# Expert stage of a graph layer with routed experts: the products of a tile with w1 set ahead of the turn of the next tile

## What is computed

```python
def _L0_ffn_ref(x, enc_w, enc_b, sw_w, sw_b, w1, b1, w2, b2):
    xt = x.reshape(-1, d)                       # 16384 tokens, d = 384
    route_prob = softmax((xt @ enc_w + enc_b) @ sw_w + sw_b)
    route_prob_max = max(route_prob)
    onehot = one_hot(argmax(route_prob), 8)
    h = einsum('td,edr->ter', xt, w1) + b1      # 64 hidden units for each expert
    h = gelu(h) * onehot[..., None]
    out = (einsum('ter,erd->td', h, w2) + onehot @ b2) * route_prob_max[:, None]
    return out
x = x + _L0_ffn_ref(_layernorm(x), ...)
```

## Time and profile before

| what | value |
|---|---|
| median of 3 runs | 2161.38 us (2161.37 to 2163.28) |
| the profiled run | 2160.51 us |
| its span, first to last instruction | 2158.7 us |
| mean granted clock of TensorE | 0.987 |
| busy: PE, DVE, ACT, POOL | 97%, 77%, 69%, 65% |

### The profile page before, as it was taken

One profiled execution on the slowest core, in us unless ns is written; L12 is line 12 of the kernel. 1 busy time (PEld: TensorE's weight loads), 2 busy tenths in 40 slices (PEclk: granted clock), 3 DMA queues, 4 the chain that ended last, 5 costly groups with the idle time before them and its releaser, 6 DMA issues. The chain is left out here.

```text
span 2158.7 us, 56998 instructions
## 1 busy us (share of the span) xinstructions
PE 2091.0 (97%) x13580; PEld 2038.0 (94%) x13581; DVE 1656.5 (77%) x5452; ACT 1491.7 (69%) x3901; POOL 1413.0 (65%) x3348
## 2 busy tenths in 40 slices
PE   6999999999999999999999999999999999968997
PEld 5999999999999999999999999999999999957996
DVE  5777777777777777677777777777777777758997
ACT  4777767667776776676776776677776767637775
POOL 2556666666666666666666666666666666655887
PEclk9999999999999999999999999999999999978999
DMA  7101111211111111111111111111111111117995
GB/s 194 32 27 50 38 49 48 104 50 47 43 49 50 51 42 50 43 47 47 43 46 50 47 42 50 44 50 50 50 39 50 47 39 49 34 56 234 279 294 192
DMA packets 94261, 153.77 MB, mean 71 GB/s; under 512 B 17621, under 2 KB 70619, under 8 KB 93954
## 3 DMA queue, kind: packets, MB, share of 16 engines
q1 hardware_dynamic: 75844, 99.61, 16.0%
q0 software_dynamic: 17408, 50.62, 6.1%
q10 hardware_dynamic: 704, 0.10, 0.0%
HBM read 96.11 MB, written 57.32 MB: 71 GB/s over the span
## 5 line engine op out<-in xcount | busy, mean ns | idle before, releaser
L422 PE MATMUL bank<-wT_hi,hT_hi 128*128 128x384 f32 x2304 | 798.8, 347 | 11.3 <-issue 4.8
L424 PE MATMUL bank<-wT_hi,hT_lo 128*128 128x384 f32 x2304 | 774.2, 336 | 0.0
L423 PE MATMUL bank<-wT_lo,hT_hi 128*128 128x384 f32 x2304 | 773.1, 336 | 0.0
L422 PEld LDWEIGHTS bank<-wT_hi,hT_hi 128*128 128x128 f32 x2304 | 434.9, 189 | 20.5 <-ACT bank L622 12.4
L423 PEld LDWEIGHTS bank<-wT_lo,hT_hi 128*128 128x128 f32 x2304 | 435.2, 189 | 0.0
L424 PEld LDWEIGHTS bank<-wT_hi,hT_lo 128*128 128x128 f32 x2304 | 434.0, 188 | 0.0
L1173 POOL TENSOR_TENSOR hT_lo<-hT,hT_hi 128x384 fp32r<-128x384 f32 x256 | 261.5, 1022 | 22.9 <-ACT hT_hi L687 21.3
L682 ACT ACTIVATE hT<-bank 128x384 f32<-128x384 f32 x256 | 125.9, 492 | 203.0 <-PE bank L414 183.5
L658 ACT CAST right_hi<-bank 128x384 fp32r<-128x384 f32 x256 | 122.6, 479 | 173.9 <-PE bank L424 173.2
L1228 POOL TENSOR_SCALAR_AFFINE_SELECT deltaT_hi<-turned_hi 128x128 fp32r<-128x128 f32 x256 | 85.3, 333 | 211.8 <-ACT turned_hi L664 209.2
L414 PE MATMUL bank<-hT 128*128 128x128 f32 x1536 | 213.3, 275 | 0.0
(11 more groups left out here) (201 smaller groups left out, 5145.2 us busy)
## 6 DMA issues: line engine op xcount, KB each, us to landing
tok<-buckets SPq DMA_DIRECT2D x72, 388.0 KB, 4.5
x_in<-in_x_dram SPq DMA_DIRECT2D x128, 192.0 KB, 2.5
x_res<-in_x_dram SPq DMA_DIRECT2D x128, 192.0 KB, 2.4
adj_in<-in_adj_dram SPq DMA_DIRECT2D x128, 64.0 KB, 2.4
buckets<-pads SPq DMA_DIRECT2D x9, 388.0 KB, 4.9
out_dram<-out_rows,row_ids POOLq DMA_INDIRECT x144
buckets<-rows,dest_words POOLq DMA_INDIRECT x128, 2.7
w_top<-in_L_ffn_w_dram SPq DMA_DIRECT2D x2, 768.0 KB
```

What stands on the lines that cost most here:

```text
L422: pe.matmul(o, hi, w_hi, start=False, stop=False, skip_group_check=True)
L423: pe.matmul(o, hi, w_lo, start=False, stop=False, skip_group_check=True)
L424: last = pe.matmul(o, lo, w_hi, start=False, stop=(c == C - 1), skip_group_check=True)
```

## The change

In TensorE's step, the products of tile i-2 with w1 are issued ahead of the transposes of tile i-1. Nothing else differs.

```diff
                     def step(i, k):
+                        if there(i - 2):
+                            hidden(i - 2, k - 2)
                         if there(i - 1):
                             turn(i - 1, k - 1)
-                        if there(i - 2):
-                            hidden(i - 2, k - 2)
                         if there(i - OUTPUT):
                             output(i - OUTPUT, (k - OUTPUT) % RING)
```

## The result

The changed kernel takes **2191.2 us** (median of 4 runs, 2190.67 to 2192.34), the kernel before beside it 2161.44: a ratio of 1.0136, interval 1.0124 to 1.0148. So it is 29.8 us slower, where 20.8 had been worked out. The profiled run took 2191.17, 1.8 above its span.

What follows compares the result with a forecast made beforehand. TensorE ran its steps without a gap, and GpSimd's store queue set the end. Steps of 2.965 against 2.678 over 68, with filling +3.5, gave +23.0; less 2.18 for stores, +20.8 us, so 2182, range 2174 to 2195.

Steps and rivals of the forecast that it cites:

- What would show it: Signs expected in the profile after: TensorE gaps 0.2 to 0.3 us, turns 2.9 to 3.0 apart, GpSimd lag near 0.9.
- The first chain: Expert-stage loop: turn's end, ScalarE's copy, w1 load, six products, next turn, closed in itself; 2.91 us a step.
- the second chain: VectorE's order over two steps, from ScalarE's copy and gelu through cast, combine, normalise, last-third copy: 5.845, 2.92 a step.
- The release of the products: Latency from a copy's end to TensorE's load of w1: 0.07 us taken, bounds 0.00 and 0.25.
- My upper bound of 0.25: Rival: every release costs 0.25, not 0.07; step 3.134 us, time 2193.5; past 2194 without a falling clock, chance 0.06.
- The turn of the loop: VectorE's loss to issue once in eight tiles: 0.35 us per eight, 0.044 a step, hidden before, exposed after.
- The filling: Pipeline start of the expert stage: first combine at 1963.2 instead of 1959.70, +3.5 us, bounds +2.2 and +4.1.
- The store queue: GpSimd's scattered stores, 2.71 us a tile, had fallen back by 2.18 us, which a slower TensorE gets back.
- The third rival: Span's end doesn't move or comes earlier; stores alone would set it if steps stayed at 2.65; chance 0.04.
- The falling clock: Rival: TensorE's clock drops to its lower level in the loop; half the steps slow gives +66, near 2248; chance 0.03.

Runs made afterwards that it cites:

- the cast's other form: Changed kernel on chip 7 with VectorE's cast of the gelu's upper part written as a two-input maximum of the gelu with itself: 2194.37 us, ratio 1.0150.
- the kernel with two products: Kernel before, on chip 14, with the third of the three products with w1 (channels 256 to 383) left out: 2221.92 us, ratio 1.0026.

## Why the prediction was right, and where its sizes were off

**The mechanism was right.** Turn, copy and products of one tile became a closed path. The gaps, the gelu straight behind the copy, the cast waiting for the gelu and the clock at 1.00 are all in the rows after, as listed under "What would show it". The first chain of 2.91 is there to the hundredth: of the 64 distances between the turns of tiles 5 to 69, 8 are within 0.01 of 2.91 in the changed kernel on chip 7, and 21 in the one without writes. Three signs of that list came otherwise. The copies didn't end TensorE's gaps in equal numbers but 48 to 16, VectorE's the more, so the second chain was the longer by more than 0.01. The turns were not 2.9 to 3.0 apart but 3.08 in the median, from 2.91 to 3.50. And GpSimd waited for the combine in 16 places, not at all tiles; its lag was 0.83 at tile 68, as expected.

**The range held by some luck.** The time is 9 us above the sum and 3.8 below the upper end. That end was worked out for a release of 0.25 us on both chains. What came was 0.22 on one of them, and a stretched cast and a later filling, for which the range had only its 2 us.

**A step: 3.080, not 2.965.** The first two of these terms of the second chain were too small.
*The release of the products.* I took 0.07 for either copy, from a row with ScalarE's. Behind ScalarE's copy it is that, mostly 0.06 to 0.07. Behind VectorE's it is mostly 0.21 to 0.23, as in the rows above: 2041.05 to 2041.28 and 2044.00 to 2044.22. The chain passes it once in two steps, so with 0.22 it is +0.075 a step: 5.845 becomes 5.995, or 3.00 a step. My upper bound of 0.25, for which I gave 0.06, was nearer the mark for that engine, but I had charged it to both chains. The cause isn't shown. In the kernel's text the wait for ScalarE's copy stands ahead of this one, and the wait for the gelu of two tiles back behind it.
*The cast.* 0.296 before, 0.360 after: +0.032 a step by the halving that the cast's other form showed. Before, 40 of the 60 casts of tiles 5 to 64 started with no store under way and none was held by one to its end; now the cast starts right behind the gelu, 58 of 60 start inside a store, and 32 end just behind it, by up to 0.29 later than alone. In the rows above the store ends at 2044.86 and the cast, 0.45 long, at 2044.98. That a moved instruction may take longer was in no term of my sum.
*The turn of the loop.* I had 0.35 per eight tiles. What is left of the step is 3.080 - 3.00 - 0.032 = 0.048, or 0.38 per eight, which is near the 2.4 us in 7 places of the waits. This term is a remainder, so it takes up what is off in the other two as well.
Together 3.080 - 2.965 = 0.115 a step, 7.8 us over 68.

**The filling: 5.3 us, not 3.5.** The turn of tile 1 took 1.46 at the lower clock where I took 0.97; I had this 0.66 as the upper bound and 0.49 of it came. The rest, 1.2, is that the products of tile 0 started at 1952.80 instead of 1951.59. ScalarE's copy of tile 0 stands behind its normalise of tile 1, and that waited for its rows until 1950.73. Nothing that the change moves comes ahead of this load, so I put it down to the run; that is argued, not shown. The changed kernel without its writes speaks for it: there the products of tile 0 start at 1951.57, and the first combine comes at 1963.80, 0.6 behind my 1963.2, of which the slow turn is 0.5. On chip 7 the first combine comes at 1963.80 to 1966.29 in the three changed kernels and at 1962.28 in the kernel before without its writes, so from one profile to another this term varies by 2.5 us in either order.

**The store queue: 2.18 predicted, 2.23 given back.** This term held, and the kernel before without its writes, with the same lag, shows that it is the time in which GpSimd issues, not that of the writes. The end of the span says the same: it comes 16.9 us behind the combine of tile 68 before and 14.9 after. The third rival fell with its condition: steps didn't stay at 2.65.

**The falling clock** is refuted for this loop: steps of 2.91 to 3.50 us with 2.65 us of work in each left it at 1.00. The Trainium skill (TensorE: Matmul & The Clock Gate, A second HAM failure mode) tells of a kernel with short idle gaps and cycled banks in which it goes back and forth; here it doesn't.

**On chip 11** the same change costs 1.0024; on chip 14 the changed kernel itself wasn't run. Nothing in the prediction covered that: it took one chip's profile for the kernel's. The median distance of turns of the changed kernel is 3.20 us on chip 11 and 3.06 on chip 7, so its path is no shorter there. The kernel before loses 54 us on that chip and the changed one 30, so the order adds little there; how the held-up tiles share this out stays open with their cause.

## What to carry to other kernels

When two engines hand a tile back and forth, put a whole other piece of work between the hand-over and its use; to move the use up to the hand-over turns cover into a closed path, and the step is then the sum of that path, whatever each engine's share of busy time was. Follow the path over two steps as well as one: here the longer chain went through VectorE's queue and was found only by walking its order. And size each term for the place to which the change moves it, since a release by another engine and a cast beside a store each cost more there than in the rows of before.

## What the runs showed of the hardware

- **TensorE's load of w1 came later behind VectorE's copy than behind ScalarE's**: mostly 0.21 to 0.23 us after the end of the one (in 37 of 48 tiles of the result's profile) and 0.06 to 0.07 after that of the other (in 12 of 16). Why isn't shown.
- **A cast on VectorE is held by the later part of a store that GpSimd issues.** A cast that starts 0.54 to 0.82 us into a store of 1.00 ends 0.11 to 0.13 after it (2044.98 and 2044.86), in 32 cases of 32. One that starts 0.41 to 0.53 into it isn't held, in 19 of 19, and an operation with two inputs runs on beside the store at any of these times. The other way round, GpSimd's row numbers, 0.21 long alone, take 0.59 to 0.62 in 28 of the 35 tiles in which VectorE's normalise starts 0.10 to 0.12 behind them (2043.10 and 2043.20), and then end 0.02 to 0.04 after it. The Trainium skill (SBUF — State Buffer, SBUF: two separate sides) calls the shared port pair an exclusive lock on which the other engine blocks, for the whole instruction. The trace agrees for these cases, and differs for the casts that run through beside the first part of a store.
- **The clock fell behind most of the long stalls.** In the changed kernel on chip 11 TensorE stood still six times for 2.3 to 3.2 us in the loop, and behind five of them the products and the next turn were slow. In one of these it stood from 1984.57 to 1987.65, and the six products behind it took 2.60 instead of 1.53:

```profile
1983.00:1987.60 4.60, 1.57 (x12) 1.00 0.77 221
1987.60:1990.20 2.60, 2.55 (x7) 0.57 0.44 172
```

(Stretch, us, TensorE's busy time, granted clock, DMA share, GB/s.) In the kernel with the copy ahead of the normalise a stall of 3.14 us had no such fall behind it: the products took 1.56.
- **Chips differ in one stage.** The kernel before took 2161.6 us on chip 7 and 2215.3 and 2215.5 on chips 14 and 11. The profiles taken there, of its neighbours, put the loss behind the stage's start: the first combine comes at 1959.92 in the kernel with two products and at 1965.04 in the changed one, as in the profiles of the kernels before and after (1959.70 and 1965.01).
